# One key/value unit between every two products with V in place of two between every four, in pairs two to four of an attention kernel on Trainium2

## What is computed

```python
qkv = x_flat @ W_qkv.T
q, k, v = (qkv[0], qkv[1], qkv[2])
var_v = jnp.var(v, axis=-1, ddof=1, keepdims=True)
var_k = jnp.var(k, axis=-1, ddof=1, keepdims=True)
scores = var_v @ jnp.swapaxes(var_k, -2, -1) * scale
attn = jax.nn.softmax(scores, axis=-1)
out = attn @ v
out = out @ W_proj.T + b_proj
x = x + out
...
x = x + displace(group_norm(x), offset)
```

## Time and profile before

| | |
|---|---|
| median of 3 runs | 2025.69 us (2025.69 to 2027.23) |
| the profiled execution | 2027.71 us |
| its span, first to last instruction | 2026.0 us |
| granted TensorE clock, mean | 0.997 of full speed |
| busy share PE / DVE / ACT / POOL | 97% / 86% / 60% / 14% |

### The profile page before, as it was taken

The page is one execution under the profiler, slowest core; times in us unless marked ns, Lnnn a source line. Parts: engine busy times, 40 slices in busy tenths (PEclk is TensorE's granted clock), DMA queues, the critical chain, the costliest instruction groups (busy, mean ns, idle before and its releaser), DMA issues.

```text
span 2026.0 us, 33485 instructions
## 1 busy us (share of the span) xinstructions
PE 1966.9 (97%) x12672; PEld 1109.0 (55%) x12672; DVE 1739.5 (86%) x3663; ACT 1206.9 (60%) x1322; POOL 276.1 (14%) x324
## 2 busy tenths in 40 slices
PE   5999989999999999999999999999999999999997
PEld 4755437563565536654375634756356553665443
DVE  7887686998779987899869998699878998599977
ACT  3667634776367762778527783477636776277820
POOL 2100001111012110111001111111101211011121
PEclk9999999999999999999999999999999999999999
DMA  8212313545235552356424562354523554134515
GB/s 331 84 54 64 105 63 87 138 141 169 85 116 158 148 177 63 116 137 185 139 64 128 152 190 86 92 139 137 167 84 118 155 154 129 43 116 137 157 42 187
DMA packets 110193, 255.19 MB, mean 126 GB/s; under 512 B 47312, under 2 KB 48080, under 8 KB 110032
## 3 DMA queue, kind: packets, MB, share of 16 engines
q0 software_dynamic: 31968, 116.41, 19.6%
q1 hardware_dynamic: 72016, 114.62, 18.7%
q10 hardware_dynamic: 6048, 22.02, 3.3%
HBM read 172.93 MB, written 79.73 MB: 125 GB/s over the span
## 4 chain that ended last, share of the span: by engine, by line
PE 60%; DVE 22%; issue 8%; DMA 5%; ACT 4%; SPq 0%; ACTq 0%; POOL 0%; DVEq 0%; POOLq 0%
PE ps L1405 23%; PE ps L1464 17%; PE ps L1447 16%; DVE bt L940 9%; DVE st L892 4%; ACT ring L714 3%; DMA a_sb<-a_rows 2%; PE ps L1422 2%; DMA a_rows<-at 2%; DVE bt L1064 1%; DVE bt L1061 1%; DVE xv L1074 1%; DVE xv L1077 1%; DVE xv L969 1%; DMA xv<-in_L_conv_W_qkv 1%
## 5 line engine op out<-in xcount | busy, mean ns | idle before, releaser
L714 ACT ACTIVATE ring<-a_sb,coef 128x1024 f32<-128x1024 f32 x768 | 817.9, 1137 | 22.9 <-issue 10.0
L1405 PE MATMUL ps<-wkv_hi,h_sp 128*128 128x256 f16 x4608 | 771.8, 273 | 12.0 <-DVE wkv_lo L1260 10.7
L1447 PE MATMUL ps<-ring,xv 128*64 128x512 f32 x3072 | 688.3, 596 | 7.5 <-ACT ring L714 6.2
L1405 PE MATMUL ps<-wkv_lo,h_sp 128*128 128x256 f16 x2304 | 628.9, 273 | 0.0
L940 DVE TENSOR_TENSOR bt<-bt,ring 128x1024 f32<-128x1024 f32 x528 | 615.3, 1214 | 3.0 <-ACT ring L714 1.9
L1405 PEld LDWEIGHTS ps<-wkv_hi,h_sp 128*128 128x128 f16 x4608 | 451.6, 98 | 91.7 <-issue 26.8
L1447 PEld LDWEIGHTS ps<-ring,xv 128*64 128x64 f32 x3072 | 209.2, 137 | 424.7 <-issue 384.1
L698 ACT ACTIVATE xv<-ps 128x256 f32<-128x256 f32 x192 | 72.6, 382 | 522.9 <-DVE st L892 522.0
L1464 PE MATMUL ps<-xv,wp_hi 128*128 128x512 f16 x1152 | 351.4, 380 | 6.2 <-DVE xv L1184 4.5
L892 DVE BATCH_NORM_STATS2 st<-ps 128x6 f32<-128x64 f32 x1536 | 218.0, 214 | 116.1 <-PE ps L1405 115.1
L1405 PEld LDWEIGHTS ps<-wkv_lo,h_sp 128*128 128x128 f16 x2304 | 225.8, 98 | 26.7
(11 more groups left out here) (174 smaller groups left out, 1349.8 us busy)
## 6 DMA issues: line engine op xcount, KB each, us to landing
a_sb<-a_rows SPq DMA_DIRECT2D x96, 512.0 KB, 4.5
out<-xv POOLq DMA_DIRECT2D x84, 512.0 KB, 5.3
xv<-in_x POOLq DMA_DIRECT2D x48, 512.0 KB, 3.6
h_sp<-in_x ACTq DMA_DIRECT2D x42, 512.0 KB, 5.1
shift_rows<-bt POOLq DMA_DIRECT2D x42, 512.0 KB, 3.4
bt<-r_rows SPq DMA_DIRECT2D x80, 256.0 KB, 4.2
bt<-in_x SPq DMA_DIRECT2D x24, 512.0 KB, 9.3
shift_rows<-ring SPq DMA_DIRECT2D x12, 528.0 KB, 15.5
```

The source lines that it names most:

```text
L714: nc.scalar.activation(ring_of(p, s, m), a_sb[:, h % 4, :], ACT.Exp, scale=coef[:, h, m:m + 1]).then_inc(s_exp, 1)
L1405: last = nc.tensor.matmul(ps[:, kv_bank[u % 2], half * 2 * P:(half + 1) * 2 * P], h_sp[:, k, hp, m * P:(m + 1) * P], wkv[wpart][:, k, q * ...
L1447: last = nc.tensor.matmul(ps[s * HD:(s + 1) * HD, o_bank[p % 2] + j, :], v_sb[:, p, m, s * HD:(s + 1) * HD], ring_of(p, s, m)[:, j * HALF: ...
```

## The change

In pairs p = 1, 2 and 3 TensorE runs one unit ahead of each of the steps 0, 2, 4 and 6, in place of two ahead of step 0 and two ahead of step 4. In pair 0 the two units ahead of step 0 stay; of the two ahead of step 4 one moves to step 6. Pair 4 stays. With the second unit of a pair now behind step 1, the transposition moves from behind step 3 to behind step 4 (p = 1 to 3), and its copy `a_out` on DVE from step 4 to step 5, past `o_normalise`. DVE's statistics of a pair's first unit move from step 3 to step 2, ahead of the addition of step 3. On ACT the four evictions move from steps 3, 3, 7, 7 to steps 2, 4, 6, 7.

```diff
@@ ACT, span @@
-                            if p <= 4:
+                            if p in (0, 4):
                                 v_evict(b, nxt)
                                 v_evict(b, nxt + 1)
+                        if 1 <= p <= 3 and m in (2, 4):
+                            v_evict(b, nxt + m // 2 - 1)
                         if m == 5 and later:
                             middle_tap_x(l1, p)
                         if m == 7:
...
                             if p <= 3:
-                                v_evict(b, nxt + 2)
+                                if p == 0:
+                                    v_evict(b, nxt + 2)
                                 v_evict(b, nxt + 3)
+                        if 1 <= p <= 3 and m == 6:
+                            v_evict(b, nxt + 2)
@@ DVE, span @@
                         if m == 3:
-                            if 1 <= p <= 4:
+                            if p == 4:
                                 kv_stats(b, nxt)
...
+                        if m == 2 and 1 <= p <= 3:
+                            kv_stats(b, nxt)
+                        if m == (4 if p == 0 else 5) and p <= 3:
+                            a_out(b, p + 1, later)
                         if m == 4:
-                            if p <= 3:
-                                a_out(b, p + 1, later)
@@ TensorE, span @@
-                        if m == 0 and p <= 4 or m == 4 and p <= 3:
+                        if p <= 3 and m % 2 == 0 and (p, m) != (0, 2):
                             kv_unit(b, nxt + m // 2, later)
-                            kv_unit(b, nxt + m // 2 + 1, later)
+                        if p == 0 and m == 0:
+                            kv_unit(b, nxt + 1, later)
+                        if p == 4 and m == 0:
+                            kv_unit(b, nxt, later)
+                            kv_unit(b, nxt + 1, later)
                         weigh(b, p, m, later, p + 1 if (p, m) == (4, 1) else None)
-                        if p <= 3 and m == 3:
+                        if p <= 3 and m == (3 if p == 0 else 4):
                             a_transpose(b, p + 1)
```

## The result

The changed kernel takes **2083.43 us** (median of 4, 2080.96 to 2088.49) beside 2026.22 for the kernel before: ratio 1.0284, 95% interval 1.0271 to 1.0297. The profiled execution is one of the four, 2085.71 us, span 2084.0, mean granted clock 0.988. The prediction was 2055 (2038 to 2076): the sign was right, the size was half of what came, and the time lies above the range.

What follows compares the result with a forecast made beforehand. TensorE, with no idle time in the changed pairs and DVE nearly as full, was taken as the bound. Borders of 2.5 us plus 3.8 us in each of seven images made 29 us on 2025.7: 2055 us, range 2038 to 2076.

Steps and rivals of the forecast that it cites:

- the borders: TensorE, switches between units and products: 0.25 us a round, pairs 1 to 3 from 31.07 to 31.8, 2.5 us an image.
- the wait at step 3: DVE in pairs 1 to 3 waits 1.5 us for an ACT eviction and one exponential ahead of step 3's additions.
- So it costs 0 at the median landing: Coefficients' rows after the later `a_out`: 0 at the median landing (6.6 against 7.6 allowed), 1.9 us a pair at worst.
- late rows: Rival: coefficients' rows reach ACT late in pairs after the moved `a_out`, 1 us for each of 21 pairs, 2076; chance 0.15.
- the sum's 29 us: Whole kernel: 2.5 us plus 3.8 us for each of seven images with layer 1 beside them.
- The prediction's own sign: Profile after, ACT: exponentials of pairs 2 to 4 start with no wait for `a_sb`.
- the bounds of 2.5 and 4.75 us: DVE's lateness at pair 4, per image: 2.5 us if all its step 3 waits are covered, 4.75 if none.
- It stays some 2.4 us behind: DVE no longer catches up with TensorE over the pairs, where before it was 0.9 us behind at pair 4.
- hardly waits: DVE at a pair's second unit: it ends at 11.6 us, DVE asks for it at 11.9; costed at nothing.
- Only the borders: Rival: DVE's wait at step 3 is covered, leaving 17 us of unit/product switches, 2043 (2036 to 2047); chance 0.20.
- Faster: Rival: waits of pairs 4 and 5 vanish and new switches cost nothing, 10.6 us less, 2015; chance 0.03.
- No change: Rival: the 20 us of unit/product switches fall wholly into existing waits; within 0.2%, chance 0.03.

Runs made afterwards that it cites:

- e10: Kernel before, with only the fourth unit of pairs 1 to 3 moved from ahead of step 4 to ahead of step 6 on TensorE: 2045.94 us, 1.0098.
- e5: Kernel before, with only statistics and eviction of the first unit moved to step 2 in pairs 1 to 3: 2057.2 us, 1.015.
- e6: Kernel before, with only the copy `a_out` of pairs 1 to 3 moved from step 4 to step 5: 2060.64 us, 1.0175.
- e2: Changed kernel, with the transposition of pairs 1 to 3 between the third unit's halves and `a_out` back in step 4: 2061.12 us, 1.017.
- e3: Changed kernel, first eviction back behind step 3's exponentials, transposition between the third unit's halves, `a_out` back in step 4 (pairs 1 to 3): 2054.75 us, 1.0137.
- e9: Kernel of e3, with the fourth unit of pairs 1 to 3 ahead of step 5 in place of step 6: 2056.26 us, 1.0147.
- e4: Changed kernel, with pair 4's transposition one step later, in step 2 in place of step 1: 2078.6 us, 1.0261.
- e8: Kernel before, with the next image's first loads moved from pair 4 and the start of pair 5 to steps 1 and 2 of pair 5: 2021.38 us, 0.9979.

## Why the prediction was wrong in size

**Right: the borders.** A pair of 31.8 was foretold and 31.84 measured; 16 products take 3.59 us, the transposition between products 0.21, one round more 0.25 (e10). 20.5 of the 57 us.

**Right: the wait at step 3.** 1.5 us foretold; 1.55 in the kernel after, 1.56 in e5, released by ACT. Alone it costs 31 us, against 7 x 3.8 = 26.6.

**Wrong: "So it costs 0 at the median landing".** This is the step that failed. The late rows stood among the rivals at 0.15 and 1 us a pair, and in the likeliest case at nothing. Alone (e6) the moved copy costs 34 us; undone (e2) it gives some 16 back beside the cheaper border. The working had ACT's need right (5.8 us after `a_out`, 6.1 foretold), but let ACT start at 7.6 and took 6.6 for the transfers, from a write of 2.1 and the landing's median of 4.5. In the 21 pairs at stake (p = 1 to 3, seven images) ACT starts 7.0 to 8.4 us after `a_out`, 7.4 at the median: 7.15 in pair 2 of image 3 (920.03 - 912.88; the write took 916.03 - 912.91 = 3.1), 8.4 in pair 1 (888.01, with the write issued at 879.60). Before, with the copy in step 4, there were 896.76 - 888.33 = 8.4 us from its end to the need.

So the transfers are longer than the step took them to be, but 17 of these 21 starts lie within the 7.6 us that were to cost nothing. The larger fault is the need: the step asked only when DVE's first additions want exponentials. Behind ACT's late start stands `d_copy` too, and behind that DVE's reciprocal; in e6 DVE waits 12.7 us more at the additions and 15.6 more at the reciprocal. And what DVE loses there TensorE loses: its denominators at the end of the pair wait for DVE (12.4 us in all, a wait that the prediction has nowhere), and in pair 4 of image 3 the reciprocal waits 1.04 ahead of the second unit's statistics, which hold the transposition: 3.50 us in place of the 2 foretold. Of the sum's 29 us 20 were borders and 9 a wait in pair 4; the waits came to 13.1 in pairs 1 to 3 and 20.7 in pair 4. The prediction's own sign told of it: ACT was to start pairs 2 to 4 with no wait for `a_sb`, and it waits at the start of all 21, 1.2 to 2.6 us each.

A slip that changes nothing: the bounds of 2.5 and 4.75 us for seven images make 2046 to 2061, not 2047 to 2065.

**Right in number, wrong in cause: DVE's lag at pair 4.** "It stays some 2.4 us behind" holds in e2, e3, e5, e9 and e10 at 2.45. The prediction gave it to the wait at step 3, and wrote that DVE "hardly waits" for the second unit: that unit ends at 11.6 us, and DVE asks for it at 11.9. But 1.5 of the 11.9 are the wait at step 3; without it DVE asks at 10.4, 1.2 us too early, and 1.21 is what e3 and e9 show once that wait is gone. The floor stood in the prediction's own numbers; that its 2.4 held all the same was luck. e10 has the lag without that wait, without late rows and with the second unit in its old place. So the lag has more than one cause: where DVE is the slower engine (e5), TensorE's denominators wait for it and it follows by what it has to do behind its last addition; where it is not (e3, e9, e10), a unit holds it; both come to 2.45 here. No run moves the second unit alone; that it suffices is read from e9's row. Causes that stand in for each other don't add: 31 and 34 alone, with borders of 20, would make 85, and 57 came.

**Missing: the clock.** The table shows 1.00 and nothing before suggested otherwise. Behind the longer wait the products run at half the clock, 11.6 us in six images. It cost little here: the stretch in which they stand grew by 2.5 us, and e4, with a shorter wait and one slow run in place of six, is 3.1 us shorter from pair 4 to the first projection. Without the waits for pair 5's rows, as in e8, the same slow products would have nothing to hide in; that was not tried.

**The rivals.** Only the borders (2043): not so; no kernel with one unit at a time in pairs 1 to 3 came below 2054. Faster: not so; no wait of TensorE's vanished except that of pair 5's products. Late rows: the right mechanism, and together with the forecast's, not in place of it. No change: not so; the borders' 20 us stand in full beside the waits.

**Open.** Which other transfers make the write and the landing in pairs 1 to 3 longer after the change (from the write's issue to the broadcast's 1.7 to 3.0 us at the median of 21 pairs, the landing 4.5 to 5.4) wasn't tried.

## What to carry to other kernels

A copy whose result goes through memory and back has a due time: before moving it, set its slack (here 8.4 us to the need, 7.0 to 8.4 for write, issue and landing) against the move (2.3 + 1.2 us), take the long landings rather than the median, and ask what else stands behind the engine that will start late. Work handed over in pairs lets the engine behind it get ahead while it waits for nothing; handed over in single pieces at even spacing, each piece can hold it, and the lead that a later stage lived on is gone. Where several parts of a change all spend the same lead, undo them one by one and together: each undone alone gives little back (8 and 22 of 57 us), and each alone costs more than half (31 and 34).

## What the runs showed of the hardware

TensorE's clock can fall behind a short wait. In the kernel after, image 3, TensorE waited 3.50 us; then the granted clock was 0.50, the lower of its two levels (1.2 in place of 2.4 GHz), for 3 us, 0.61 as a mean over the next 3 us, and 1.00 after that, with TensorE busy all the while. Behind a wait of 0.46 us (e4) it stayed at 1.00. Waits of 1.91 us had both outcomes: in e10 the 44 products were slow in six images of seven (11.36 us in the row of image 3, against 9.66 in the earlier trace rows), in e2 and e9 in four, in e5 in three, in e3 in two. In image 4 of the kernel after they were not slow behind 3.33 us. What tells these cases apart is open.
